# Exchanging two PSUM evacuations between VectorE and ScalarE in the attention stage, and issuing three loads earlier

## The chip, the cores and the metric

One Trainium2 chip; the same program runs on eight of its cores, each on its own 1,024 of 8,192 rows of x. The metric is the device time of the slowest core in microseconds.

## The reference

Per row of x (4,096 wide), with xn the layer norm of x:

```
c  = conv1d(xn, width 3, 4096 -> 3072) + conv_b ; q, k, v = split(c)      # each 1024 wide
qh, kh, vh = q wq + bq, k wk + bk, v wv + bv                              # 16 heads of 64
p  = softmax(causal(qh kh^T / 8))     within blocks of 128 rows
s  = ((p vh) wo + bo) proj_w + proj_b                                      # 4096 wide
w  = top-8 of softmax(xn rw^T + rb), 64 experts
g  = silu(xn * sum(w) + w expert_bias)
out = x + s * g
```

## The kernel before

The program is written out by hand: every `@PE`, `@DV`, `@AC`, `@GP`, `@SY` function adds a piece to the instruction stream of TensorE, VectorE (DVE), ScalarE (ACT), GpSimd (POOL) or SyncE (SP), in the order of the text, and the engines meet only at semaphores.

Stages, one after the other: layer norm, transposes and router (to about 210 us), convolution (to about 1,220 us, L632 and L647), the three projections q, k, v (L682, L694, L716, L726, to about 1,308 us), attention (L755 to L924, 1,308 to 1,576 us), final projection with gate and output (L965 to the end).

Attention has 8 blocks of 128 rows and 16 heads. A unit of work Q is four heads of one block, so Q runs from 0 to 31; eight consecutive Q (two blocks) form a block pair `bp`, and there are four pairs. For each Q:

- `st_quad` (PE, L755 and L758): scores of four heads into half of pS, then the mask is added by one more matmul. Semaphore cS.
- `st_dve1` (DVE, L765): negated row maximum. cNM.
- `st_exp` (ACT, L772): Exp with that maximum as bias, in place in pS. cEXP.
- `st_dve2` (DVE, L779, L783, L787): row sums, reciprocal, four multiplies that write bf16. cPS.
- `st_pt` (PE, L799): transposes into pPT. cPT.
- `st_pte` (ACT, L809): copies pPT to SBUF (pTs). cPTe.
- `st_ot` (PE, L823): four matmuls with vh into pOT. cOT.
- `st_ote` (DVE, L839): four tensor_scalar adds of the bias bv, 64x128 each, into oT2. cOTe.

Within a pair the step of Q puts these on the engines, in this order. PE: quad(Q), pt(Q-1), ot(Q-2). DVE: dve2(Q-1), dve1(Q), and after them ote(Q-3). ACT: pte(Q-2), exp(Q). After the last Q of a pair (Qm) come dve2(Qm), the last copies pte(Qm-1) and pte(Qm), the last pt and ot, and three ote. Only then do the 128 matmuls of the output projection of that pair (L913, pWO) start, since they wait for all its ote (cOTe); ACT evacuates them in eight instructions (L924, cEV5), counted on the PE side by cPE5. pS, pPT and pOT have two halves each, used by Q modulo 2.

Every `@AC` function that has ACTIVATE instructions shows one ACT_TABLE_LOAD in the trace.

Around the end of attention: POOL loads proj_w in eight pieces (L602, pw), the first when cS reaches 32 (the quad of Q = 31 is done), each next one when the piece before it has landed. SP waits at L934 for cEV5 = 32 and cOT = 32, loads proj_b (L936, into the first row of x6[0]'s buffer), waits at L937 for cPB = 2 (proj_b split into a high and a low bf16 part by ACT L945 and DVE L950), and then loads the x of tile 0 and tile 1 (L938 and L939, 2 MB each, x6[0] and x6[1]). PE starts L965 at cPB = 2 and takes one proj_w piece after another. The last tiles are paced by x loads that are issued one tile ahead (L1071).

Of the kernel before, what the change touches and what calls it, by code (L numbers as in the profile page):

```python
# [9 lines left out]
AF = mybir.ActivationFunctionType  # L10
ALU = mybir.AluOpType
# [71 lines left out]
def build_program():  # L83
    nc = bass.Bass("TRN2", target_bir_lowering=False)

    d_x = nc.dram_tensor("x", [NT + 2, D], F32, kind="ExternalInput").ap()
# [21 lines left out]
    with contextlib.ExitStack() as es:  # L108
        def sb(name, shape, dt):
            return es.enter_context(nc.sbuf_tensor(name, shape, dt))  # L110
# [7 lines left out]
        t_bvT = sb("tBvT", [64, 16], F32)  # L118
# [17 lines left out]
        def bfv(off, cols, parts=128):  # L136
            return AL[0:parts, off:off + cols]

        def f32v(off, cols_f32, parts=128):
            return AL[0:parts, off:off + 2 * cols_f32].bitcast(F32)  # L140
# [38 lines left out]
        pTs = bfv(A_PT, 1024)  # L179
        pbf = bfv(A_PBF4, 1024)  # L180
        x6 = [f32v(A_X6A, 4096), f32v(A_X6B, 4096)]
# [64 lines left out]
        SY, GP, PE, DV, AC = blk.sync, blk.gpsimd, blk.tensor, blk.vector, blk.scalar  # L246
# [15 lines left out]
        @SY  # L262
        def _(e):
            sCONST.add(e.dma_start(out=t_cbT[:], in_=d_cb), 16)
            sCONST.add(e.dma_start(out=t_bqT[:], in_=d_bq), 16)
            sCONST.add(e.dma_start(out=t_bkT[:], in_=d_bk), 16)
            sCONST.add(e.dma_start(out=t_bvT[:], in_=d_bv), 16)
            sCONST.add(e.dma_start(out=t_boT[:], in_=d_bo), 16)
            sCONST.add(e.dma_start(out=t_rbT[:], in_=d_rb), 16)
            sCONST.add(e.dma_start(out=i64v, in_=d_i64), 16)  # L270
            sCONST.add(e.dma_start(out=i128f, in_=d_i128), 16)
            sXA.add(e.dma_start(out=xA[0:64, :], in_=d_rw), 16)
# [463 lines left out]
        with nc.psum_tensor("pS", [128, 2 * 512], F32) as p_S, \  # L736
# [7 lines left out]
            def st_quad(e, Q):  # L744
                b, qi = divmod(Q, 4)
                sB = 512 * (Q % 2)
                if Q == 0:
                    e.wait_ge(cEV3.h, EV3ALL)
                    e.wait_ge(sCST2.h, 48)
                if Q >= 2:  # L750
                    e.wait_ge(cPS.h, 4 * (Q - 1))
                for i in range(4):
                    head = 4 * qi + i
                    off = 1024 * head + 128 * b
                    e.matmul(p_S[:, sB + 128 * i:sB + 128 * i + 128],  # L755
                             qhT[:, off:off + 128], khT[:, off:off + 128],
                             start=(i == 0), stop=False)
                cS.add(e.matmul(p_S[:, sB:sB + 512], t_i128[:], t_mask4[:],  # L758
                                start=False, stop=True), 1)

            def st_dve1(e, Q):
                e.wait_ge(cS.h, Q + 1)
                if Q >= 2:
                    e.wait_ge(cEXP.h, Q - 1)
                cNM.add(e.reduce_max(nmax[Q % 2][:],  # L765
                                     p_S[:, 512 * (Q % 2):512 * (Q % 2) + 512],
                                     axis=AX.X, negate=True), 1)

            def st_exp(e, Q):
                e.wait_ge(cNM.h, Q + 1)  # L770
                sB = 512 * (Q % 2)
                cEXP.add(e.activation(p_p[:, sB:sB + 512], p_S[:, sB:sB + 512],  # L772
                                      AF.Exp, bias=nmax[Q % 2][:]), 1)
# [30 lines left out]
            def st_pte(e, Q):  # L804
                e.wait_ge(cPT.h, Q + 1)
                if Q >= 2:
                    e.wait_ge(cOT.h, Q - 1)
                sB = 512 * (Q % 2)
                cPTe.add(e.activation(pTs[:, sB:sB + 512], p_pT[:, sB:sB + 512],  # L809
                                      AF.Copy), 1)  # L810

            def st_ot(e, Q):
                b, qi = divmod(Q, 4)
# [16 lines left out]
            def st_ote(e, Q):  # L830
                b, qi = divmod(Q, 4)
                e.wait_ge(cOT.h, Q + 1)
                if b // 2 >= 2:
                    e.wait_ge(cPE5.h, 8 * (b // 2 - 1))
                sB = 512 * (Q % 2)
                dst = oT2[(b // 2) % 2]
                for i in range(4):
                    head = 4 * qi + i
                    cOTe.add(e.tensor_scalar(  # L839
                        dst[0:64, head, 128 * (b % 2):128 * (b % 2) + 128],  # L840
                        p_oT[0:64, sB + 128 * i:sB + 128 * i + 128],
                        t_bvT[:, head:head + 1], None, ALU.add), 1)

            for bp in range(4):
                Qs = list(range(8 * bp, 8 * bp + 8))
                for Q in Qs:
                    @PE
                    def _(e, Q=Q, Qs=Qs):
                        st_quad(e, Q)
                        if Q - 1 in Qs:  # L850
                            st_pt(e, Q - 1)
                        if Q - 2 in Qs:
                            st_ot(e, Q - 2)

                    @DV
                    def _(e, Q=Q, Qs=Qs):
                        if Q - 1 in Qs:
                            st_dve2(e, Q - 1)
                        st_dve1(e, Q)

                    @AC
                    def _(e, Q=Q, Qs=Qs):
                        if Q - 2 in Qs:
                            st_pte(e, Q - 2)
                        st_exp(e, Q)

                    @DV
                    def _(e, Q=Q, Qs=Qs):
                        if Q - 3 in Qs:
                            st_ote(e, Q - 3)  # L870

                Qm = Qs[-1]

                @DV
                def _(e, Qm=Qm):
                    st_dve2(e, Qm)

                @AC
                def _(e, Qm=Qm):
                    st_pte(e, Qm - 1)  # L880

                @PE
                def _(e, Qm=Qm):
                    st_pt(e, Qm)
                    st_ot(e, Qm - 1)

                @AC
                def _(e, Qm=Qm):
                    st_pte(e, Qm)

                @PE
                def _(e, Qm=Qm):
                    st_ot(e, Qm)

                @DV
                def _(e, Qm=Qm):
                    st_ote(e, Qm - 2)
                    st_ote(e, Qm - 1)
                    st_ote(e, Qm)

                @PE
                def _(e, bp=bp, Qm=Qm):
                    e.wait_ge(cOTe.h, 32 * (bp + 1))
                    if bp == 0:
                        e.wait_ge(sWO.h, 16)
                    src = oT2[bp % 2]
                    for c in range(8):
                        wB = 512 * (c % 2)
                        if c >= 2:
                            e.wait_ge(cEV5.h, 8 * bp + c - 1)  # L910
                        ins = None
                        for hk in range(16):
                            ins = e.matmul(p_wo_t[:, wB:wB + 256],  # L913
                                           wob[:, hk, 128 * c:128 * c + 128],
                                           src[0:64, hk, 0:256],
                                           start=(hk == 0), stop=(hk == 15))
                        cPE5.add(ins, 1)

                @AC
                def _(e, bp=bp):  # L920
                    for c in range(8):
                        e.wait_ge(cPE5.h, 8 * bp + c + 1)
                        wB = 512 * (c % 2)
                        cEV5.add(e.activation(aoT[:, c, 256 * bp:256 * bp + 256],  # L924
                                              p_wo_t[:, wB:wB + 256], AF.Identity,
                                              bias=t_boT[:, c:c + 1]), 1)
# [4 lines left out]
        with nc.psum_tensor("pPr", [128, 8 * 512], F32) as p_pr:  # L931
            @SY
            def _(e):
                e.wait_ge(cEV5.h, 32)  # L934
                e.wait_ge(cOT.h, 32)
                sPB32.add(e.dma_start(out=pbf32, in_=d_pb), 16)  # L936
                e.wait_ge(cPB.h, 2)  # L937
                sX6A.add(e.dma_start(out=x6[0], in_=d_x[1:129, :]), 16)  # L938
                sX6B.add(e.dma_start(out=x6[1], in_=d_x[129:257, :]), 16)  # L939

            @AC
            def _(e):
                e.wait_ge(sPB32.h, 16)
                e.wait_ge(cEV5.h, 32)
                cPB.add(e.copy(pbhi[0:1, :], pbf32[0:1, :]), 1)  # L945

            @DV
# [212 lines left out]
if __name__ == "__main__":  # L1160
    nc = build_program()
    print("instructions:", nc.n_instructions())
```

## Time and profile before

| | |
|---|---|
| median of 2 runs | 1893.26 us (1889.58 and 1896.95) |
| profiled execution | 1901.35 us; span of its slowest core 1899.8 us |
| spans of the eight cores in it | 1869.2 to 1899.8 us |
| busy share of the span, PE / DVE / ACT / POOL | 81% / 21% / 20% / 12% |
| attention stage in the span | about 1,308 to 1,576 us |

The shares are averages over stages with different limits: PE is at nine tenths or more through the convolution, and at five to eight tenths in the slices of attention and of the final projection. So the attention stage has to be read in its own timeline, by the start of one operation that recurs in each step, and by what ends each wait. In a timeline row the bracket gives the idle time of that engine before the instruction and what ended it.

### The profile page before, as it was taken

The numbers are of one execution on the slowest core, as the hardware profiler recorded it, in microseconds if no ns is written. First come the engines' busy times: TensorE is split into PE (matmuls) and PEld (weight loads), VectorE is DVE, ScalarE is ACT, GpSimd is POOL, SyncE is SP. The second block draws the span as 40 slices with busy tenths as digits, with TensorE's granted clock in tenths as the row PEclk, the third lists the DMA queues.
The fourth block names the chain that finished last, engine by engine and source line by source line (L and its number), as shares of the span: only waits on it lengthen the run. The fifth ranks groups of instructions, "written<-read, shape, count | busy, mean of one in ns | idle before, by whom it ended". The sixth has DMA issues, their size and how long they took to land.

```text
span 1899.8 us, 17839 instructions; the slowest of 8 cores (1869.2 to 1899.8 us)
## 1 busy us (share of the span) xinstructions
PE 1534.9 (81%) x7424; PEld 726.5 (38%) x7424; DVE 393.7 (21%) x644; ACT 383.6 (20%) x453; POOL 229.3 (12%) x180
## 2 busy tenths in 40 slices
PE   0344799999999999999999999887756775876771
PEld 0344344444444444444444444333434442221220
DVE  2776200000000000000000000002354241454664
ACT  1443000000000000000000000496354341423322
POOL 0000111111111111111111111000000000132343
PEclk9867899999999999999999999997555556887775
DMA  5998666666666666666666666522000037134234
GB/s 138 213 244 167 78 78 75 72 76 77 78 78 76 72 74 78 78 78 76 74 74 77 78 78 73 94 48 41 1 1 1 1 69 182 27 123 142 89 99 167
DMA packets 230821, 163.62 MB, mean 86 GB/s; under 512 B 74691, under 2 KB 222403, under 8 KB 226499
## 3 DMA queue, kind: packets, MB, share of 16 engines
q0 software_dynamic: 155472, 92.97, 38.6%
q1 hardware_dynamic: 75270, 69.50, 14.1%
q8 instruction: 60, 0.98, 0.2%
q14 instruction: 19, 0.16, 0.0%
HBM read 220.69 MB, written 16.78 MB: 125 GB/s over the span
## 4 chain that ended last, share of the span: by engine, by line
PE 61%; DMA 12%; DVE 9%; ACT 7%; POOL 4%; issue 3%; SPq 3%; POOLq 0%; DVEq 0%; ACTq 0%
PE pCv L632 53%; DMA AL<-x 7%; PE pWO L913 4%; DMA AL<-pw 4%; POOL AL L1050 2%; ACT AL L694 2%; POOL AL L1053 2%; SPq L416 2%; DVE AL L787 1%; PE pQ L716 1%; DVE tStat L320 1%; DVE tRs L779 1%; ACT L694 1%; DVE tSc L765 1%; DVE AL L839 1%
## 5 line engine op out<-in xcount | busy, mean ns | idle before, releaser
L632 PE MATMUL pCv<-AL 128*128 128x512 bf16 x4608 | 1000.6, 379 | 1.0 <-DVE tWmT L550 1.0
L632 PEld LDWEIGHTS pCv<-AL 128*128 128x128 bf16 x4608 | 449.5, 98 | 551.9 <-issue 1.3
L765 DVE TENSOR_REDUCE tSc<-pS 128x1 f32<-128x512 f32 x32 | 21.8, 682 | 1187.7 <-PE pS L758 1187.7
L575 POOL DMA_DIRECT2D AL<-cw x144 | 125.9, 875 | 1054.0 <-PE pCv L632 860.6
L647 ACT ACTIVATE AL<-pCv,tCbT 128x512 bf16<-128x512 f32 x48 | 29.1, 688 | 889.2 <-PE pCv L632 889.2
L454 PE MATMUL pLgT<-AL 128*64 128x128 bf16 x768 | 60.3, 258 | 129.3 <-DMA AL<-AL 129.3
L982 PE MATMUL pPr<-AL 128*128 128x512 bf16 x448 | 120.9, 418 | 22.3 <-DVE AL L1030 22.3
L913 PE MATMUL pWO<-AL 64*128 64x256 bf16 x512 | 109.8, 416 | 5.7 <-DVE AL L839 5.7
L454 PEld LDWEIGHTS pLgT<-AL 128*64 128x64 bf16 x768 | 59.3, 138 | 130.2 <-issue 130.2
L913 PEld LDWEIGHTS pWO<-AL 64*128 64x128 bf16 x512 | 74.5, 146 | 40.1 <-issue 6.6
L982 PEld LDWEIGHTS pPr<-AL 128*128 128x128 bf16 x448 | 42.2, 104 | 96.8 <-issue 63.5
L799 PE MATMUL pPT<-tI,AL 128*128 128x128 bf16 x128 | 18.7, 300 | 72.9 <-DVE AL L787 72.9
L1050 POOL TENSOR_TENSOR AL<-AL 128x1536 f32<-128x1536 f32 x8 | 45.5, 5686 | 187.8 <-ACT AL L1042 187.8
L682 PE MATMUL pQ<-AL 128*128 128x512 bf16 x256 | 57.7, 379 | 10.3 <-ACT AL L694 7.5
L1011 PE MATMUL pPr<-AL,tWmT 64*128 64x512 bf16 x64 | 29.5, 562 | 36.7 <-ACT AL L1001 36.7
L320 DVE BATCH_NORM_STATS2 tStat<-AL 128x6 f32<-128x512 f32 (+1 forms) x72 | 43.5, 677 | 17.8 <-DMA AL<-x 17.8
L1060 DVE TENSOR_TENSOR AL<-AL 128x2560 f32<-128x2560 f32 x8 | 45.9, 5741 | 2.5 <-ACT AL L1044 2.5
L1030 DVE TENSOR_TENSOR AL<-AL,pPr 128x512 f32<-128x512 f32 x64 | 39.0, 680 | 32.7 <-PE pPr L1011 31.6
L799 PEld LDWEIGHTS pPT<-tI,AL 128*128 128x128 bf16 x128 | 11.1, 126 | 87.2 <-issue 87.2
L602 POOL DMA_DIRECT2D AL<-pw x8 | 4.3, 533 | 327.6 <-PE pS L758 258.8
L965 PE MATMUL pPr<-AL 128*128 128x512 bf16 x64 | 20.0, 486 | 29.1 <-DMA AL<-pw 29.1
L1025 DVE TENSOR_SCALAR AL<-AL,tMrv,tSc 128x4096 f32<-128x4096 f32 x8 | 19.3, 2413 | 114.2 <-DMA AL<-x 114.0
(95 smaller groups left out, 878.4 us busy)
## 6 DMA issues: line engine op xcount, KB each, us to landing
AL<-cw POOLq DMA_DIRECT2D x144, 512.0 KB, 5.9
AL<-x SPq DMA_DIRECT2D x16, 2048.0 KB, 15.9
out<-AL SPq DMA_DIRECT2D x8, 2048.0 KB, 9.1
AL<-pw POOLq DMA_DIRECT2D x8, 1024.0 KB, 8.5
AL<-wq POOLq DMA_DIRECT2D x1, 2048.0 KB, 19.8
AL<-wk POOLq DMA_DIRECT2D x1, 2048.0 KB, 15.9
AL<-wv POOLq DMA_DIRECT2D x1, 2048.0 KB, 15.7
AL<-wo POOLq DMA_DIRECT2D x1, 2048.0 KB, 16.4
```

The source lines that it names most:

```text
L320: ins = e.bn_stats(t_stat[rows, sb0 + 6 * c:sb0 + 6 * c + 6], xt[rows, 512 * c:512 * c + 512])
L454: ins = e.matmul(p_lgT[:, 128 * j:128 * j + 128], lhsT_t[:, 64 * dcc:64 * dcc + 64], src_[:, o:o + 128], start=(j % 4 == 0 and p == 0 and ...
L575: sCWs[gi % 4].add(e.dma_start(out=cwr[:, gi % 4, :].rearrange("p (g f) -> p g f", g=8), in_=d_cw[s, g].rearrange("g p f -> p g f")), 16)
L632: ins = e.matmul(p_cv[:, 512 * (bs + 2 * sub + hf): 512 * (bs + 2 * sub + hf) + 512], lhsT, xnTh[:, o:o + 512], start=(step == 0), stop=(s ...
L682: ins = e.matmul(p_q3[:, 512 * (bs + hf):512 * (bs + hf) + 512], lhsT, cvT[:, 8 * m + kc, 512 * hf:512 * hf + 512], start=(kc == 0), stop= ...
L694: cEV3.add(e.activation(outT[0:64, 1024 * head + 512 * hf: 1024 * head + 512 * hf + 512], p_q3[64 * hh:64 * hh + 64, 512 * (bs + hf):512 * ...
L765: cNM.add(e.reduce_max(nmax[Q % 2][:], p_S[:, 512 * (Q % 2):512 * (Q % 2) + 512], axis=AX.X, negate=True), 1)
L913: ins = e.matmul(p_wo_t[:, wB:wB + 256], wob[:, hk, 128 * c:128 * c + 128], src[0:64, hk, 0:256], start=(hk == 0), stop=(hk == 15))
L982: e.matmul(p_pr[:, 512 * seg:512 * seg + 512], aoT[:, kc, 128 * tt:128 * tt + 128], pwv[:, kc, 512 * seg:512 * seg + 512], start=(kc == 0) ...
L1030: cGI.add(e.tensor_add(gw[:, 512 * seg:512 * seg + 512], gw[:, 512 * seg:512 * seg + 512], p_pr[:, 512 * seg:512 * seg + 512]), 1)
L1050: cPL.add(e.tensor_mul(s6[tt % 2][:, 0:1536], s6[tt % 2][:, 0:1536], gw[:, 0:1536]), 1)
L1060: dedge(e, e.tensor_mul(s6[tt % 2][:, 1536:4096], s6[tt % 2][:, 1536:4096], gw[:, 1536:4096]))
```

## The change

`st_pte`, the copy of pPT to SBUF, goes from ACT (activation Copy) to DVE (tensor_copy). `st_ote`, the four bias adds, go from DVE (tensor_scalar) to ACT (activation Identity with a bias pointer). The order within a step becomes: DVE dve2(Q-1), dve1(Q), pte(Q-2); ACT exp(Q), ote(Q-3). At the end of a pair, the two last copies are on DVE and the three last ote are one function on ACT.

SP's waits for cEV5 and cOT at L934 become one for cPE3 = 24 (the last matmul of the q, k, v projections); proj_b and x6[1] are loaded right behind it, and x6[0] alone stays behind cPB = 2. ACT's split of proj_b waits for cPE5 = 32 in place of cEV5 = 32.

```diff
--- before.py
+++ after.py
@@ -806,8 +806,7 @@
                 if Q >= 2:
                     e.wait_ge(cOT.h, Q - 1)
                 sB = 512 * (Q % 2)
-                cPTe.add(e.activation(pTs[:, sB:sB + 512], p_pT[:, sB:sB + 512],
-                                      AF.Copy), 1)
+                cPTe.add(e.tensor_copy(pTs[:, sB:sB + 512], p_pT[:, sB:sB + 512]), 1)
 
             def st_ot(e, Q):
                 b, qi = divmod(Q, 4)
@@ -836,10 +835,10 @@
                 dst = oT2[(b // 2) % 2]
                 for i in range(4):
                     head = 4 * qi + i
-                    cOTe.add(e.tensor_scalar(
+                    cOTe.add(e.activation(
                         dst[0:64, head, 128 * (b % 2):128 * (b % 2) + 128],
                         p_oT[0:64, sB + 128 * i:sB + 128 * i + 128],
-                        t_bvT[:, head:head + 1], None, ALU.add), 1)
+                        AF.Identity, bias=t_bvT[:, head:head + 1]), 1)
 
             for bp in range(4):
                 Qs = list(range(8 * bp, 8 * bp + 8))
@@ -857,15 +856,12 @@
                         if Q - 1 in Qs:
                             st_dve2(e, Q - 1)
                         st_dve1(e, Q)
+                        if Q - 2 in Qs:
+                            st_pte(e, Q - 2)
 
                     @AC
                     def _(e, Q=Q, Qs=Qs):
-                        if Q - 2 in Qs:
-                            st_pte(e, Q - 2)
                         st_exp(e, Q)
-
-                    @DV
-                    def _(e, Q=Q, Qs=Qs):
                         if Q - 3 in Qs:
                             st_ote(e, Q - 3)
 
@@ -874,9 +870,6 @@
                 @DV
                 def _(e, Qm=Qm):
                     st_dve2(e, Qm)
-
-                @AC
-                def _(e, Qm=Qm):
                     st_pte(e, Qm - 1)
 
                 @PE
@@ -884,7 +877,7 @@
                     st_pt(e, Qm)
                     st_ot(e, Qm - 1)
 
-                @AC
+                @DV
                 def _(e, Qm=Qm):
                     st_pte(e, Qm)
 
@@ -892,7 +885,7 @@
                 def _(e, Qm=Qm):
                     st_ot(e, Qm)
 
-                @DV
+                @AC
                 def _(e, Qm=Qm):
                     st_ote(e, Qm - 2)
                     st_ote(e, Qm - 1)
@@ -931,17 +924,16 @@
         with nc.psum_tensor("pPr", [128, 8 * 512], F32) as p_pr:
             @SY
             def _(e):
-                e.wait_ge(cEV5.h, 32)
-                e.wait_ge(cOT.h, 32)
+                e.wait_ge(cPE3.h, 24)
                 sPB32.add(e.dma_start(out=pbf32, in_=d_pb), 16)
+                sX6B.add(e.dma_start(out=x6[1], in_=d_x[129:257, :]), 16)
                 e.wait_ge(cPB.h, 2)
                 sX6A.add(e.dma_start(out=x6[0], in_=d_x[1:129, :]), 16)
-                sX6B.add(e.dma_start(out=x6[1], in_=d_x[129:257, :]), 16)
 
             @AC
             def _(e):
                 e.wait_ge(sPB32.h, 16)
-                e.wait_ge(cEV5.h, 32)
+                e.wait_ge(cPE5.h, 32)
                 cPB.add(e.copy(pbhi[0:1, :], pbf32[0:1, :]), 1)
 
             @DV
```

## Rows read from the trace of the kernel before

**Rows 1.** Page, part 4, shares of the chain that ended last, by line.
```profile
PE pCv L632 53%; DMA AL<-x 7%; PE pWO L913 4%; DMA AL<-pw 4%; POOL AL L1050 2%; ACT AL L694 2%; POOL AL L1053 2%; SPq L416 2%; DVE AL L787 1%; PE pQ L716 1%; DVE tStat L320 1%; DVE tRs L779 1%; ACT L694 1%; DVE tSc L765 1%; DVE AL L839 1%
```

**Rows 2.** Timeline, fourth block pair, its first two steps: start, us, engine, line, operation [idle].
```profile
1509.80 0.69 DVE L765 TENSOR_REDUCE tSc<-pS 128x1 f32<-128x512 f32 x1 [28.75 <-PE pS L758]
...
1514.82 0.68 DVE L765 TENSOR_REDUCE tSc<-pS 128x1 f32<-128x512 f32 x1
...
1515.58 1.28 ACT L772 ACT_TABLE_LOAD   x1 [3.05 <-DVE tSc L765]
...
1516.87 0.66 ACT L772 ACTIVATE pS<-pS,tSc 128x512 f32<-128x512 f32 x1
...
1519.83 0.68 DVE L765 TENSOR_REDUCE tSc<-pS 128x1 f32<-128x512 f32 x1
```

**Rows 3.** Timeline, the same pair, one later step.
```profile
1534.97 0.68 DVE L765 TENSOR_REDUCE tSc<-pS 128x1 f32<-128x512 f32 x1
...
1535.57 1.11 DVE L839 TENSOR_SCALAR AL<-pOT,tBvT 64x128 bf16<-64x128 f32 x4
...
1535.75 0.66 ACT L772 ACTIVATE pS<-pS,tSc 128x512 f32<-128x512 f32 x1 [1.23 <-DVE tSc L765]
...
1535.82 0.64 PE L823 MATMUL pOT<-AL 128*64 128x128 bf16 x4
...
1536.43 1.28 ACT L809 ACT_TABLE_LOAD   x1
...
1536.60 0.67 DVE L779 TENSOR_REDUCE tRs<-pS 128x4 f32<-128x512 f32 x1
...
1537.73 1.13 DVE L787 TENSOR_SCALAR AL<-pS,tRr 128x128 bf16<-128x128 f32 x4 [0.18 <-DVE tRr L783]
...
1538.78 0.68 DVE L765 TENSOR_REDUCE tSc<-pS 128x1 f32<-128x512 f32 x1
```

**Rows 4.** Timeline, the end of that pair.
```profile
1546.56 1.12 DVE L839 TENSOR_SCALAR AL<-pOT,tBvT 64x128 bf16<-64x128 f32 x4 [1.20 <-PE pOT L823]
...
1547.82 27.46 PE L913 MATMUL pWO<-AL 64*128 64x256 bf16 x128 [1.44 <-DVE AL L839]
```

**Rows 5.** Groups by shape: line, engine, operation, shapes, count, busy us, mean ns, idle.
```profile
L809 ACT ACT_TABLE_LOAD x32 | 41.1, 1283 | 6.5 <-PE pPT L799 6.1
...
L772 ACT ACT_TABLE_LOAD x8 | 10.3, 1283 | 18.0 <-DVE tSc L765 18.0
...
L647 ACT ACTIVATE AL<-pCv,tCbT 128x512 bf16<-128x512 f32 x48 | 29.1, 688 | 889.2 <-PE pCv L632 889.2
...
L694 ACT ACTIVATE AL<-pQ,tBqT 64x512 bf16<-64x512 f32 x32 | 21.9, 683 | 0.7
...
L924 ACT ACTIVATE AL<-pWO,tBoT 128x256 bf16<-128x256 f32 x32 | 15.2, 474 | 77.2 <-PE pWO L913 77.2
...
L489 DVE COPY AL<-pLgt 128x512 f32<-128x512 f32 x1 | 0.7, 691 | 2.2 <-PE pLgt L481 2.2
```

**Rows 6.** Chain that ended last, in order of time: start, us, what.
```profile
1538.11 9.10 DMA AL<-pw
...
1565.16 8.10 DMA AL<-pw
...
1592.10 17.95 DMA AL<-pw
...
1610.58 10.33 DMA AL<-pw
...
1621.05 3.37 PE pPr L965 x8
```

**Rows 7.** Timeline between the fourth pair and the projection.
```profile
1575.99 0.22 SPq L936 DMA_DIRECT2D AL<-pb  x1
...
1581.58 1.28 ACT L945 ACT_TABLE_LOAD   x1 [5.72 <-DMA AL<-pb]
...
1591.07 0.37 SPq L938 DMA_DIRECT2D AL<-x  x1
```

## The prediction

> **What bounds the kernel now.** I read the page first, its chain that ended last. Convolution matmuls are 53% of it and the change does not touch them; the rest is many small shares, of which the proj_w load has 4% and the attention lines one or two per cent each [rows 1]. So the change acts on attention (some 267 us) and on the loads behind it, and I read both in the timeline, by the start of dve1 (L765), once per step.
>
> Two lengths of a step stand in one block pair. The second step takes 1519.83 - 1514.82 = 5.01 us, the first 5.02 [rows 2]. In it nothing overlaps: dve1 ends at 1515.50, ACT starts a table load at 1515.58, Exp starts at 1516.87, and DVE can only sum when Exp is over. A later step takes 1538.78 - 1534.97 = 3.81 us [rows 3]: Exp starts 0.10 after dve1 ends, since the load of that ACT function stands at its first ACTIVATE, the copy of pPT, which comes before Exp and runs while DVE is busy with dve2. DVE has no gap to speak of there; the four ote adds (1.11 us) fill the time in which it would wait for Exp.
>
> The reader is to see in the groups by shape where the loads stand: 32 at L809 (once per copy) and only 8 at L772, for the two steps of each of four pairs that begin with Exp [rows 5]. The load at L772 begins after the wait for dve1, not during it: its row has 3.05 us idle that ended with tSc L765 [rows 2].
>
> Behind attention the chain runs through the proj_w pieces: the first is issued at 1538.11, when quad 31 is done, the last is issued at 1610.58 and lands for PE at 1621.05 [rows 6]. The seventh took 17.95 us where others take 8.1 to 9.1, because the two x loads were issued at 1591.07 and right after [rows 7], 4 MB on the same DMA engines.
>
> **The change part by part.** *Copy to DVE, ote to ACT, the load ahead of Exp.* Now Exp is the first ACTIVATE of every ACT function in a step, so the load stands between dve1 and Exp in all eight steps of a pair. The serial path of a step is then that of [rows 2]: 5.01 us. I take this value, since it is a measured step of the same kernel with the same order dve1, load, Exp, dve2, dve1. The Trainium skill says of the compiler's loads that they are placed per block (ScalarE activation tables: per-element evaluation and per-set limits, section Table sets in the compiler and the runtime); the counts in [rows 5] agree.
>
> The copy on DVE costs about 0.69, by a DVE copy of 128x512 f32 out of PSUM [rows 5] (that one writes f32; bf16 is not shown to be slower). It lies between dve1(Q) and dve2(Q), where DVE waits over 2.0 us for load and Exp (1516.87 + 0.66 - 1515.50): hidden. If that cover were gone it would cost 0.69 a step.
>
> Four Identity with bias, 64x128 each: no such row. 128x256 takes 474 ns and 128x512 688 ns, so 0.84 ns a column; 64 partitions cost as much as 128 (683 ns) [rows 5]. For 128 columns: 474 - 107 = 367 ns, with a small gap 0.385, four are 1.54 us. The bounds: from below what DVE takes for the same four, 1.11 us or 0.28 each [rows 3]; from above the 474 ns of twice the columns. ACT in a step: 0.08 + 1.28 + 0.67 + 1.54 = 3.6 us, under 5.01; even four at 474 ns give 3.9. Hidden in the steady part. What is queued behind it is Exp of the next step, due 5.01 later. On PE, ot(Q-2) now waits for a copy that ends 0.7 after dve1(Q); quad(Q+1) queued behind it ends at most 3.9 us after the start of dve1(Q) (0.68 + 0.69 + 0.2 + 2.3, the last from the fourth-pair sum below) and is wanted at 5.01: 1.1 us spare.
>
> Sum of a pair: seven intervals of dve1. Before 1538.78 - 1509.80 = 28.98 [rows 2, 3]; after 7 x 5.01 = 35.07; +6.1 us.
>
> *The end of a pair.* Before, from the last dve1 (1538.78) to the first pWO matmul (1547.82) 9.04 us [rows 3, 4]. After, counted from that dve1: load and Exp until 0.76 + 1.28 + 0.67 = 2.71; ote(Qm-3) until 4.25; the load of the last ACT function until 5.55; three ote of 1.54 until 10.17; pWO 0.14 later (before, it came 0.14 after the end of ote), 10.3. The pOT of Qm is ready earlier, at about 7.8, where it was before (ote began at 1546.56, 7.78 after [rows 4]): the load before the last copy is gone, one before Exp has come. So +1.3 us, ACT bound. With 0.28 for one Identity ote ends at 7.8 + 1.11 and pWO starts at 9.05: 0; with 0.474, 11.65: +2.6.
>
> *Three pairs* lie ahead of the fourth: 3 x (6.1 + 1.3) = +22.2 us. The bounds of the tail make this 18.3 to 26.1.
>
> *Fourth pair.* What counts is quad 31, since it releases proj_w. Its predecessor on PE is the pOT group of the copy. Before, that group started at 1535.82 and POOL issued 2.29 later, at 1538.11, 28.31 after the pair's start [rows 2, 3, 6]. After: dve1 of Q = 30 starts at 6 x 5.01 = 30.06, ends 30.74, copy until 31.43, pOT at 31.65, issue at 33.95. +5.6 us. Sum at the first proj_w piece: +27.8 us (bounds 24 to 32).
>
> *The early loads.* proj_b and x6[1] go out at about 1,308 us, with the v projection done and only attention running, which loads nothing by then but proj_w at its end: no cost. The proj_b split no longer waits the 5.6 us for its load (1575.99 to 1581.58), so it is done 9.5 us after attention's last evacuation (1591.07 - 1581.58) [rows 7]; PE does not gain by it, as the proj_w pieces bound PE. x6[0] alone now meets the sixth or seventh piece. Two x loads made the seventh 17.95 instead of about 8.4, +9.5, and the eighth 10.33, part of it theirs. Half the bytes, half of it: about -5 us. Bounds: 0 (one load costs all) and -9.5 (the one left is hidden).
>
> *ACT's wait on cPE5 = 32*: nothing; it stands behind L924 in ACT's order anyhow. From the last proj_w piece to the end nothing changes: the x loads there keep their order.
>
> Sum: +27.8 - 5 = +22.8 us. On the profiled execution, 1901.35 becomes 1924.1; that execution is 8 us above the median, so on the median 1893.3 becomes 1916.1 us, +1.2%.
>
> **The rivals.** *Loads off the path.* If the loads ran during the wait, or only when the table set changes, a step would be 5.01 - 1.28 = 3.73 us, against 3.81. Then the DVE's lighter work shows: 5 x 0.08 in a pair, 1.6 us in all, at the tails about 1.3 less each (5 us), and the 5 of the x load: 1882 us, faster than before, not slower. It decides in the first three steps of a pair. For it: both functions of a step may share a set, as Copy and Exp do (one load for both). Against it: the load is repeated each step though the same two functions alternate, and it starts after the wait. 7%.
>
> *A second load, for Identity after Exp.* No row shows the two in one function. ACT in a step would be 3.6 + 1.28 = 4.9, still under 5.01, and each tail 1.3 longer: three times, +4: 1920 us. Its upper end: Identity at 474 ns as well makes ACT 5.2 a step and Exp late by 0.2: +6 more. The Trainium skill says that cheap functions, identity among them, are in every set (ScalarE: Activation LUTs, section Table sets: the hidden batching unit), which speaks against it. 8%.
>
> *ACT becomes the bound.* If an Identity of 128 columns cost as much as one of 512 (0.69) and a second load came, ACT would need 0.08 + 1.28 + 0.67 + 1.28 + 2.76 = 6.1 us a step: 27 steps at +1.1 and tails +5 each, 1960 us, slower by over 2%. It decides where four Identity exceed 1.7 us with a second load, or 3.0 without one. Against it the slope of [rows 5]. 5%.
>
> *A pause behind each load.* In the trace Exp begins 0.01 us after the load ends (1515.58 + 1.28 = 1516.86) [rows 2]. With a pause as long as the load behind each, 27 steps on the path (7 in each of three pairs, 6 in the fourth) would add 27 x 1.28 = 35 us, 1951 us. That is what the Trainium skill gives for a switch of set, 1283 ns plus a drain of about 1380 (ScalarE: Activation LUTs, section What ACT_TABLE_LOAD costs). The load's 1283 ns agree with [rows 5], the drain does not appear in [rows 2]. 1%.
>
> *The early x load brings nothing*, because the load that stays costs as much as both: 1921 us. 9%.
>
> **How the numbers follow.** The forecast has 70%: 1916 us, own range 1906 to 1923 (tail bounds -4 and +4, load bounds, and a few us between executions, as the two runs before are 7 apart). With the second load and the useless early load its upper end is 1926; the faster rival stays outside below. The range is 1904 to 1926. A measurement of this kernel can tell about 2% from no change, 38 us: 1855 and 1931. Faster by over 2% 1%, since no case reaches it; slower by over 2% 8%: the bound on ACT, the pause, and the top of the second load; within 2% 91%.
>
> **What would show it.** Right: 32 table loads at L772 and none at the copy; dve1 starting every 5.0 us through a whole pair; 1.3 to 1.5 us of DVE idle before each row sum, after the copy; pWO 45 us after the first dve1 of a pair, where it was 38; the seventh proj_w piece near 13 us. Wrong: steps of 3.7 us; table loads between Exp and Identity; Identity above 0.45 us; ACT without idle time; a first proj_w piece less than 24 us later than before.

## The result and the profile after

The changed kernel takes 1912.6 us (median of 11 executions) where the kernel before takes 1890.3 in the same sessions; the ratio is 1.0106, with a 95% interval of 1.0060 to 1.0151. So it is about 20 us slower: the whole interval lies above 1, though the size is under the 2% that I took as the smallest difference to call. The forecast was 1.2%.

In the profiled execution of the changed kernel, cores 2 and 3 lost some 50 us in the convolution, which the change does not touch, at a lower granted clock (0.838 over the span, core 5 0.859). All rows of it below are therefore of core 5. The lines of the kernel after have other numbers than those before: the copy stays L809, but ote is L838 (before L839), ot L822 (L823), the output projection L906 (L913), its evacuation L917 (L924).

The groups by shape on core 5 (line, engine, operation, shapes, count | busy us, mean ns | idle before, releaser):

```profile
L772 ACT ACT_TABLE_LOAD x32 | 41.1, 1283 | 76.5 <-DVE tSc L765 76.5
...
L838 ACT ACTIVATE AL<-pOT,tBvT 64x128 bf16<-64x128 f32 x128 | 35.6, 355 | 2.0 <-PE pOT L822 1.9
...
L838 ACT ACT_TABLE_LOAD x4 | 5.1, 1283 | 0.1
...
L917 ACT ACT_TABLE_LOAD x4 | 5.1, 1283 | 15.3 <-PE pWO L906 15.3
```

These answer to [rows 5]. Of the 40 table loads of the attention steps, 32 stood at the copy and 8 at Exp; now there are 36: 32 stand at Exp (L772), all behind a wait for dve1 (76.5 us of idle time, released by tSc), and 4 at the three last ote (L838), one for each pair. None stands between Exp and Identity.

One step of the first pair in the timeline on core 5 (start, us, engine, line, operation [idle before]):

```profile
1330.29 0.68 DVE L765 TENSOR_REDUCE tSc<-pS 128x1 f32<-128x512 f32 x1
...
1330.89 0.68 DVE L809 CAST AL<-pPT 128x512 bf16<-128x512 f32 x1
...
1331.05 1.28 ACT L772 ACT_TABLE_LOAD   x1 [2.01 <-DVE tSc L765]
...
1331.85 0.61 PE L822 MATMUL pOT<-AL 128*64 128x128 bf16 x4 [0.65 <-DVE AL L809]
...
1332.34 0.66 ACT L772 ACTIVATE pS<-pS,tSc 128x512 f32<-128x512 f32 x1
...
1332.93 1.11 ACT L838 ACTIVATE AL<-pOT,tBvT 64x128 bf16<-64x128 f32 x4
...
1333.10 0.69 DVE L779 TENSOR_REDUCE tRs<-pS 128x4 f32<-128x512 f32 x1 [1.54 <-ACT pS L772]
...
1334.25 1.13 DVE L787 TENSOR_SCALAR AL<-pS,tRr 128x128 bf16<-128x128 f32 x4 [0.18 <-DVE tRr L783]
...
1335.30 0.68 DVE L765 TENSOR_REDUCE tSc<-pS 128x1 f32<-128x512 f32 x1
```

It answers to [rows 3]. The step is 1335.30 - 1330.29 = 5.01 us, where it was 3.81, and equal to the second step of [rows 2]. After dve1 comes the load, then Exp, and DVE waits 1.54 us for them in spite of the copy (0.68) that now fills part of that time. The four Identity take 1.11 us and end long before ACT is wanted again.

The end of that pair, on the same core:

```profile
1345.66 0.68 DVE L765 TENSOR_REDUCE tSc<-pS 128x1 f32<-128x512 f32 x1
...
1346.42 1.28 ACT L772 ACT_TABLE_LOAD   x1 [2.37 <-DVE tSc L765]
...
1349.43 1.28 ACT L838 ACT_TABLE_LOAD   x1
...
1350.72 1.12 ACT L838 ACTIVATE AL<-pOT,tBvT 64x128 bf16<-64x128 f32 x4
...
1352.30 2.23 ACT L838 ACTIVATE AL<-pOT,tBvT 64x128 bf16<-64x128 f32 x8 [0.46 <-PE pOT L822]
...
1354.78 15.52 PE L906 MATMUL pWO<-AL 64*128 64x256 bf16 x72 [1.47 <-ACT AL L838]
```

From the last dve1 to pWO it is 9.12 us, where [rows 3, 4] gave 9.04 for the fourth pair. The same pair on the same core took 9.09 before, so the end of a pair is as long as it was. ACT waits 0.46 us for pOT ahead of the last eight Identity, so ACT alone does not bound it.

The first, sixth, seventh and eighth proj_w pieces, on core 5 (the bracket of a row is the time that the piece before it took, so 11.82 belongs to the sixth and 9.29 to the seventh):

```profile
1563.63 0.56 POOL L602 DMA_DIRECT2D AL<-pw  x1 [284.26 <-PE pS L758]
...
1608.00 0.53 POOL L602 DMA_DIRECT2D AL<-pw  x1 [8.28 <-DMA AL<-pw]
...
1620.35 0.53 POOL L602 DMA_DIRECT2D AL<-pw  x1 [11.82 <-DMA AL<-pw]
...
1630.17 0.53 POOL L602 DMA_DIRECT2D AL<-pw  x1 [9.29 <-DMA AL<-pw]
```

They answer to [rows 6]: 1563.63 less the 1534.61 of the same core before is 29 us, of which 25.4 belong to attention on this core and the rest to the earlier stages of the two executions. The sixth and seventh together take 21.1 us, two undisturbed ones 16.7; before, the two from the sixth on took 8.4 and 17.4 on this core.

### The profile page after: what moved, and what is told of

It is laid out like the page before. It is cut to its first block, busy times and chain, and to the rows that moved or that the text cites. A ratio compares the mean times of both kernels' runs of the same rounds, so it can differ in the third digit from the quotient of the medians.

```text
span 1945.7 us, 17834 instructions; the slowest of 8 cores (1886.8 to 1945.7 us)
## 1 busy us (share of the span) xinstructions
PE 1588.0 (82%) x7424; PEld 739.1 (38%) x7424; DVE 381.2 (20%) x548; ACT 393.5 (20%) x545; POOL 229.3 (12%) x180
## 4 chain that ended last, share of the span: by engine, by line
PE 63%; DMA 10%; ACT 8%; DVE 7%; POOL 4%; issue 4%; SPq 3%; POOLq 0%; DVEq 0%; ACTq 0%
PE pCv L632 54%; DMA AL<-x 6%; PE pWO L906 4%; DMA AL<-pw 4%; POOL AL L1042 2%; ACT AL L694 2%; POOL AL L1045 2%; PE pQ L716 1%; DVE tStat L320 1%; SPq L416 1%; DVE AL L787 1%; ACT L694 1%; DVE tSc L765 1%; DVE tRs L779 1%; ACT pS L772 1%
## 5 line engine op out<-in xcount | busy, mean ns | idle before, releaser
L632 PE MATMUL pCv<-AL 128*128 128x512 bf16 x4608 | 1054.3, 394 | 1.0 <-DVE tWmT L550 1.0
L632 PEld LDWEIGHTS pCv<-AL 128*128 128x128 bf16 x4608 | 462.2, 100 | 593.1 <-issue 177.7
L974 PE MATMUL pPr<-AL 128*128 128x512 bf16 x448 | 117.8, 410 | 11.4 <-DVE AL L1022 11.4
L906 PE MATMUL pWO<-AL 64*128 64x256 bf16 x512 | 109.8, 415 | 5.7 <-ACT AL L838 5.7
L906 PEld LDWEIGHTS pWO<-AL 64*128 64x128 bf16 x512 | 73.2, 144 | 41.3 <-issue 6.5
L682 PE MATMUL pQ<-AL 128*128 128x512 bf16 x256 | 57.7, 379 | 10.3 <-ACT AL L694 7.5
L1042 POOL TENSOR_TENSOR AL<-AL 128x1536 f32<-128x1536 f32 x8 | 45.5, 5687 | 160.4 <-ACT AL L1034 160.4
L772 ACT ACT_TABLE_LOAD x32 | 41.1, 1283 | 76.5 <-DVE tSc L765 76.5
L320 DVE BATCH_NORM_STATS2 tStat<-AL 128x6 f32<-128x512 f32 (+1 forms) x72 | 43.6, 677 | 16.7 <-DMA AL<-x 16.6
L1045 POOL TENSOR_TENSOR AL<-AL 128x1536 f32<-128x1536 f32 x7 | 42.0, 5999 | 0.0
## 6 DMA issues: line engine op xcount, KB each, us to landing
AL<-wv POOLq DMA_DIRECT2D x1, 2048.0 KB, 15.7
```

Source lines behind the costliest of these rows:

```text
L320: ins = e.bn_stats(t_stat[rows, sb0 + 6 * c:sb0 + 6 * c + 6], xt[rows, 512 * c:512 * c + 512])
L632: ins = e.matmul(p_cv[:, 512 * (bs + 2 * sub + hf): 512 * (bs + 2 * sub + hf) + 512], lhsT, xnTh[:, o:o + 512], start=(step == 0), stop=(s ...
L682: ins = e.matmul(p_q3[:, 512 * (bs + hf):512 * (bs + hf) + 512], lhsT, cvT[:, 8 * m + kc, 512 * hf:512 * hf + 512], start=(kc == 0), stop= ...
L906: ins = e.matmul(p_wo_t[:, wB:wB + 256], wob[:, hk, 128 * c:128 * c + 128], src[0:64, hk, 0:256], start=(hk == 0), stop=(hk == 15))
L974: e.matmul(p_pr[:, 512 * seg:512 * seg + 512], aoT[:, kc, 128 * tt:128 * tt + 128], pwv[:, kc, 512 * seg:512 * seg + 512], start=(kc == 0) ...
L1042: cPL.add(e.tensor_mul(s6[tt % 2][:, 0:1536], s6[tt % 2][:, 0:1536], gw[:, 0:1536]), 1)
```

## A measure that the convolution does not disturb

The spans of the cores differ by more than the effect, for two reasons outside it: the convolution (up to 50 us) and the last stage, which takes anything from 238 to 269 us in kernels with the same instructions there, nearly alike within a pair of cores. So beside each ratio I give three stretches from the POOL rows of the profiled execution, medians over eight cores: **A** from the issue of the wo load to the first proj_w piece (the last 32 us of the projections, then attention up to quad 31; it is the same on all cores within 0.4 us), **B** from there to POOL's first gate multiplication, **C** from there to the end of the span.

| kernel | A us | B us | C us | ratio to before (95%) |
|---|---|---|---|---|
| before | 259.7 | 96.6 | 247.2 | |
| changed | 284.9 | 89.2 | 243.2 | 1.0106 (1.0060 to 1.0151) |
| e1 early loads only | 259.7 | 92.1 | 250.9 | 0.9975 (0.9938 to 1.0012) |
| e2 exchange only | 284.9 | 97.3 | 244.5 | 1.0141 (1.0075 to 1.0207) |
| e3 ote ahead of Exp | 262.1 | 91.5 | 263.9 | none |
| e10 the same, again | 262.1 | 91.4 | 241.1 | 1.0011 (0.9968 to 1.0054) |
| e4 one ACT function a pair | 251.7 | 90.3 | 255.7 | 0.9951 (0.9928 to 0.9974) |
| e5 before, Exp ahead of copy | 295.8 | 97.6 | 241.5 | 1.0267 (1.0217 to 1.0316) |
| e6 before, one ACT function | 250.7 | 94.4 | 241.3 | 0.9965 (0.9921 to 1.0010) |
| e8 both x loads early | 259.6 | 86.5 | 242.0 | 0.9968 (0.9923 to 1.0012) |
| e9 last stage, one function | 259.7 | 94.1 | 218.9 | 0.9896 (0.9813 to 0.9979) |
| e7 all together | 249.0 | 85.4 | 219.5 | 0.9765 (0.9708 to 0.9822) |

## Experiments: the two parts of the change apart

**Early loads only** (e1). The kernel before with SP's and ACT's new waits (ACT's, on cPE5, is not shown):

```diff
-                e.wait_ge(cEV5.h, 32)
-                e.wait_ge(cOT.h, 32)
+                e.wait_ge(cPE3.h, 24)
                 sPB32.add(e.dma_start(out=pbf32, in_=d_pb), 16)
+                sX6B.add(e.dma_start(out=x6[1], in_=d_x[129:257, :]), 16)
                 e.wait_ge(cPB.h, 2)
                 sX6A.add(e.dma_start(out=x6[0], in_=d_x[1:129, :]), 16)
-                sX6B.add(e.dma_start(out=x6[1], in_=d_x[129:257, :]), 16)
```

> The kernel before with the second part of the change alone: proj_b and x6[1] loaded behind the q, k, v projections, ACT's wait on cPE5. Theory (the load that stays costs about half of what two cost): attention steps stay at 3.81 us, the sixth and seventh proj_w pieces together exceed two undisturbed ones by 4 to 5 us in place of 9 to 10, and the kernel is 4 to 6 us faster than before (about 0.3%). Rival (one x load delays proj_w as much as two): 0 us. Rival (the early x load costs something in attention): POOL's wait for the first proj_w piece grows above 258.8 us.

A is unchanged to 0.1 us, so the early load costs attention nothing. B is 4.5 us shorter. The ratio, 0.9975, says the same size (4.7 us) but its interval includes 1.

**The exchange only** (e2). The changed kernel with SP and ACT waiting as before.

> The changed kernel with the loads as before: only the exchange of the two evacuations. Theory: steps of 5.01 us, POOL's wait from the last weight load to the first proj_w piece 284 us (before 258.8), seventh proj_w piece near 17.5 us again, and 25 us slower than before (1.3%). If the early loads were worth nothing, the same time as the changed kernel.

A is 25.2 us longer than before, the same as in the changed kernel; B is 97.3, as before. The ratio is 1.0141, +27 us. So the two parts add: one costs 25 us, the other gives 5 to 8 back.

**Both x loads early** (e8), to see whether the disturbance goes with the bytes. proj_b gets a buffer of its own, so that x6[0] need not wait for it. Shown is the difference to e1:

```diff
-        pbf32 = f32v(A_X6A, 4096, 1)
+        pbf32 = f32v(A_SA, 4096, 1)
...
+                sX6A.add(e.dma_start(out=x6[0], in_=d_x[1:129, :]), 16)
                 sX6B.add(e.dma_start(out=x6[1], in_=d_x[129:257, :]), 16)
-                e.wait_ge(cPB.h, 2)
-                sX6A.add(e.dma_start(out=x6[0], in_=d_x[1:129, :]), 16)
```

> The kernel before with both x loads and proj_b behind the projections (proj_b in a buffer of its own), so no x load meets proj_w. Theory (the disturbance goes with the bytes): all proj_w pieces at 8 to 9 us; from the first proj_w piece to the first gate multiplication 87 us, against 96.7 before and 92 with one load early; 8 us faster than before. Rival (proj_w does not bound the start of the final stage once one load is early): 92 us as with one.

B is 96.6, 92.1 and 86.5 us with two, one and no x load beside proj_w: -4.5 and then -5.6. With none, POOL's rows (core 0) show all pieces alike:

```profile
1590.09 0.53 POOL L602 DMA_DIRECT2D AL<-pw  x1 [8.83 <-DMA AL<-pw]
...
1598.93 0.53 POOL L602 DMA_DIRECT2D AL<-pw  x1 [8.32 <-DMA AL<-pw]
```

The rival, that proj_w no longer bounds the start of the last stage, falls. The ratio is 0.9968, 6 us where 8 were expected, and its interval just includes 1; that the loads help rests on B. There all twelve rows of the table agree: 94.1 to 97.6 us with both x loads beside proj_w (five kernels), 89.2 to 92.1 with one (five), 86.5 and 85.4 with none.

## Experiments: what lengthens the step

My theory is that the table load ahead of Exp sets the step. The rivals are the exchange itself (the copy in DVE's order, PE's wait for it, Identity on ACT) and a second load for Identity.

**ote ahead of Exp** (e3, and once more as e10). All instructions stay on their engines; only ACT's order changes:

```diff
-                        st_exp(e, Q)
                         if Q - 3 in Qs:
                             st_ote(e, Q - 3)
+                        st_exp(e, Q)
```

> The changed kernel with one exchange in ACT's order: in each step ote(Q-3) comes ahead of exp(Q). The same instructions on the same engines; only the place of the table load moves, to the first ote. Theory (the load ahead of Exp is what costs): the load runs while DVE does dve2 and dve1, steps with an ote ahead last 3.7 to 3.9 us and only the first three of a pair 5.0; POOL's wait falls from 284 to about 263 us, and the kernel is 0 to 3 us faster than the one before. Rival (the copy on DVE, or PE's wait for it, is what lengthens the step): steps stay near 5.0 us and the time near that of the changed kernel (+1.1%).

> The kernel with ote(Q-3) ahead of exp(Q) once more, with more rounds, for a ratio: attention 2.5 us longer than before (262.1 against 259.7 us from the wo load to the first proj_w piece), the early loads 5 us shorter: 2 to 3 us faster than before, ratio 0.998 to 0.999.

The starts of dve1 in the first pair (timeline, DVE, core 0 of e3), third to sixth:

```profile
1350.07 0.68 DVE L765 TENSOR_REDUCE tSc<-pS 128x1 f32<-128x512 f32 x1
...
1355.08 0.68 DVE L765 TENSOR_REDUCE tSc<-pS 128x1 f32<-128x512 f32 x1
...
1358.81 0.68 DVE L765 TENSOR_REDUCE tSc<-pS 128x1 f32<-128x512 f32 x1
...
1362.54 0.68 DVE L765 TENSOR_REDUCE tSc<-pS 128x1 f32<-128x512 f32 x1
```

The third step, without an ote, still takes 5.01 us; from the fourth on a step takes 3.73. A falls from 284.9 to 262.1 us: 22.8 of the 25.2 us are back through the place of one instruction. The four executions of e3 lie too far apart for a ratio (1897.8 to 2096.6 us); e10 gives 1.0011 with an interval from 0.9968 to 1.0054, which neither confirms the 2 to 3 us of gain that I expected nor excludes them. A and B are as expected.

**One ACT function for a pair** (e4). The changed kernel, order unchanged, with the eight steps and the last three ote in one function (shown are the added lines; the nine functions that they replace go):

```diff
+                @AC
+                def _(e, Qs=Qs, bp=bp):
+                    for Q in Qs:
+                        st_exp(e, Q)
+                        if Q - 3 in Qs:
+                            st_ote(e, Q - 3)
+                    for Q in Qs[-3:]:
+                        st_ote(e, Q)
```

> The changed kernel with all attention steps of a pair written into one ACT function, in unchanged order. Theory (one table load per function, none needed between Exp and Identity): one load for a pair in place of nine, every step 3.73 us (5.01 - 1.28), and the end of the pair 1.3 us shorter than before; per pair 7 x 3.73 - 28.98 = -2.9 and -1.3, so three pairs and the start of proj_w give -15 us against before, with the early loads -20 us (1.0% faster). Rival (a load for each change between Exp and Identity): two loads a step, steps of 5 us or more. Rival (the exchange itself costs): steps above 4 us without a load on the path.

Groups by shape on ACT, and two starts of dve1 with the Exp and Identity between them (core 6):

```profile
L772 ACT ACT_TABLE_LOAD x4 | 5.1, 1283 | 5.9 <-DVE tSc L765 5.9
...
L838 ACT ACTIVATE AL<-pOT,tBvT 64x128 bf16<-64x128 f32 x128 | 35.2, 357 | 7.9 <-PE pOT L822 7.6 <-issue 0.3
```

```profile
1327.47 0.68 DVE L765 TENSOR_REDUCE tSc<-pS 128x1 f32<-128x512 f32 x1
...
1328.25 0.66 ACT L772 ACTIVATE pS<-pS,tSc 128x512 f32<-128x512 f32 x1 [2.03 <-DVE tSc L765]
...
1328.84 1.11 ACT L838 ACTIVATE AL<-pOT,tBvT 64x128 bf16<-64x128 f32 x4
...
1331.20 0.68 DVE L765 TENSOR_REDUCE tSc<-pS 128x1 f32<-128x512 f32 x1
```

One load a pair, none for Identity, and a step of 3.73 us = 5.01 - 1.28, with the copy on DVE and ote on ACT. Both rivals fall: with the exchange and no load on the path a step takes 3.73, except the last of each pair (4.08). The kernel is 0.5% faster than before. I had expected 1.0%: A fell by 8.0 us against before and not by 15, because the one load of the pair stands behind the first dve1, so the first step stays at 4.95 to 5.02 (1.28 a pair forgotten), and one step of seven takes 4.08.

That last step is 0.35 us longer in every kernel with the exchange (5.36 beside 5.01 in the changed kernel and e2, 4.08 beside 3.73 in e3, e10 and e4) and in none with the evacuations as before and the copy ahead of Exp. In the changed kernel its row sum starts 1.11 us after Exp does, and 0.76 in the other steps, though the Exp row is as long (0.66). What delays it is not shown.

**The load ahead of Exp with no exchange** (e5). The kernel before, in which only the copy and Exp change places in ACT's order:

```diff
-                        if Q - 2 in Qs:
-                            st_pte(e, Q - 2)
                         st_exp(e, Q)
+                        if Q - 2 in Qs:
+                            st_pte(e, Q - 2)
```

> The kernel before with one exchange in ACT's order and nothing else: exp(Q) ahead of pte(Q-2). The copy stays on ACT, ote on DVE, the loads late. Theory (the place of the table load sets the step, whichever engine has which evacuation): every step at least 5.0 us; here the copy comes 2.04 us after dve1 instead of at once, so pOT and quad(Q+1) behind it on PE end near 5.3 us after the start of dve1(Q), and the step is 5.3 to 5.4. POOL's wait for proj_w about 290 us (before 258.8), the kernel about 30 us slower than before (1.6%). Rival (the exchange of engines is what costs): steps of 3.8 us, no change.

Two steps in DVE's timeline (core 7):

```profile
1322.40 0.69 DVE L765 TENSOR_REDUCE tSc<-pS 128x1 f32<-128x512 f32 x1 [0.25 <-PE pS L758]
...
1327.64 0.69 DVE L765 TENSOR_REDUCE tSc<-pS 128x1 f32<-128x512 f32 x1
...
1333.00 0.69 DVE L765 TENSOR_REDUCE tSc<-pS 128x1 f32<-128x512 f32 x1 [0.25 <-PE pS L758]
```

Steps of 5.24 and 5.36 us, some of them ended by PE (0.25 us for the scores, as expected from the late copy), and a kernel 2.7% slower than before, without any exchange. The direction and the step are as expected; A grew by 36 us and not by 31. The trace shows where: the seven steps of a pair are 7.8 to 8.05 us longer than before, which makes 23.7 in three pairs; from the last dve1 to pWO it is 10.2 to 10.3 us in place of 9.0 to 9.1, another 3.6, which I had not counted; and the fourth pair up to the first proj_w piece takes 37.2 in place of 28.3.

**One ACT function, before's assignment** (e6), the same edit as e4 on the kernel before.

> The kernel before, its copies still on ACT and its ote on DVE, with the ACT steps of a pair in one function; late loads. Theory: one load a pair, waiting for the first dve1, so a first step of 5.0 us, a second of 3.73, and the rest at 3.81, where DVE is busy throughout; the end of the pair 1.3 us shorter. Per pair -1.3 and -1.3, with the fourth POOL's wait falls by 9 us to about 250 us; the kernel 9 us faster than before (0.5%). Beside the same with the exchange (250.9 us measured), the exchange itself is worth 0 to 2 us once the loads are out of the way.

A is 250.7 us; with the exchange (e4) it was 251.7. So once the loads are out of the way the exchange is worth nothing, or costs 1 us. Steps are 3.80 us with ote on DVE and 3.73 without, but the last step of a pair with the exchange is the 4.08 of e4, which takes the gain back. The ratio, 0.9965, includes 1 by a hair.

## Experiments: the version that beats both

**All together** (e7): e4, both x loads early, and the same merging of ACT functions in the q, k, v projections and in the last stage (the functions are collected in a list and called in one):

```diff
-                @AC
+                @acl.append
                 def _(e, tt=tt):
...
+            @AC
+            def _(e):
+                for f in acl:
+                    f(e)
```

> The changed kernel, the ACT steps of a pair in one function, the ACT parts of the q, k, v projections in one function (16 steps of 4.12 us bound by ACT with a load of 1.28 each, PE needs 3.61: about -7.5 us), those of the final stage in one function (a load before each silu lies on the chain of each tile: up to -9 us), and both x loads early with proj_b in a buffer of its own (-3 us more). With the 9 us that the one-function version of attention gained: 1862 to 1868 us, 1.5% faster than before. If Silu and Copy share no set, the loads of the final stage stay and 9 us of it do not come.

Its ratio is 0.9765 (0.9708 to 0.9822), 44 us faster than before, which is 16 us more than the 1.5% that I expected. The projections gave 11.3 us (from the wk load to the first dve1 88.5 us, before 99.8; expected 7.5). A is 2.7 us shorter than in e4 because it holds the last of these; attention itself gave the 8 us of e4. B is 11.2 us shorter, where 5 and 3 were expected. The last stage gave most of the surplus: C fell from 247.2 to 219.5, where I had put 9 us; compared between cores whose x loads took equally long (see the last section), it fell by about 21.

**The last stage alone** (e9), on the kernel before.

> The kernel before with the ACT parts of the final stage in one function, nothing else. In the version with everything together a tile of the final stage took 28.2 us on a core where it took 31.8 before: 1.3 us for the table load ahead of the silu, and 2.55 us because POOL's first multiplication then runs in 3.45 us, ahead of DVE's, in place of 6.00 beside it. Expected here: tiles 3.5 us shorter, the stage 20 to 25 us shorter, the kernel 1.1 to 1.3% faster than before. If the shorter tiles came from the other edits of that version, only 9 us.

C is 218.9 us on every core within 3.4, and the ratio 0.9896, just short of the 1.1 to 1.3% expected. So the gain is of that stage. One tile of it before, on core 6 (timeline):

```profile
1746.01 1.28 ACT L1042 ACT_TABLE_LOAD   x1 [4.09 <-DVE AL L1030]
...
1747.30 1.49 ACT L1042 ACTIVATE AL<-AL 128x1536 f32<-128x1536 f32 x1
...
1748.84 2.82 DVE L1035 TENSOR_TENSOR AL<-AL 128x2560 f32<-128x2560 f32 x1
...
1748.93 6.00 POOL L1050 TENSOR_TENSOR AL<-AL 128x1536 f32<-128x1536 f32 x1 [19.79 <-ACT AL L1042]
...
1754.90 6.00 POOL L1053 TENSOR_TENSOR AL<-AL 128x1536 f32<-128x1536 f32 x1
...
1760.97 0.34 SPq L1071 DMA_DIRECT2D out<-AL  x1
```

And in e9, on the same core:

```profile
1763.32 1.48 ACT L1044 ACTIVATE AL<-AL 128x1536 f32<-128x1536 f32 x1 [6.05 <-DVE AL L1032]
...
1764.95 3.44 POOL L1052 TENSOR_TENSOR AL<-AL 128x1536 f32<-128x1536 f32 x1 [19.32 <-ACT AL L1044]
...
1766.14 4.94 DVE L1037 TENSOR_TENSOR AL<-AL 128x2560 f32<-128x2560 f32 x1
...
1768.36 6.00 POOL L1055 TENSOR_TENSOR AL<-AL 128x1536 f32<-128x1536 f32 x1
...
1774.43 0.34 SPq L1073 DMA_DIRECT2D out<-AL  x1
```

Before, DVE's addition starts 0.09 us ahead of POOL's multiplication, which then takes 6.00 us. Without the load POOL starts 1.19 us ahead of DVE; it takes 3.44 and DVE's takes 4.94 where it took 2.82. POOL is on the chain of the tile and DVE's addition (L1035, in e9 L1037) is not: the store of the finished tile, and behind it the x load for the next, goes out 0.07 us after POOL's second row ends in both kernels. So the load was worth 1.28 + 2.56 = 3.84 us a tile, and most tiles are that much closer: 31.8 us apart before, 27.9 to 29.3 in e9, where the longer ones wait longer for x. The Trainium skill says that DVE and GpSimd share one pair of SBUF ports under an exclusive lock, that a DVE instruction with two SBUF inputs contends for it with a GpSimd instruction that reads SBUF, and that the order of issue decides who is blocked (SBUF — State Buffer, section Who interferes with whom). These rows agree: POOL loses 2.56 us where DVE's addition has 2.73 still to run when POOL starts, and in e9 DVE loses 2.12 us where POOL has 2.25 still to run.

## Why the prediction was right

- **The load ahead of Exp, 5.01 us a step**: right, and shown from three sides. Taking the load away (e4) or moving it (e3) removes the 1.28 us, and moving it there without the exchange (e5) brings it. A step measured in the kernel before was the right price. The last step of each pair took 5.36, which I had not foreseen and no run explains.
- **One load for Exp and Identity**: right; the 8% rival of a second load is out, since L838 has 4 loads, each at the head of a function. The pause behind the load is out too: Exp starts 1.29 us after the load does.
- **Copy 0.69, hidden**: measured 0.68, hidden.
- **The tail, +1.3 us a pair**: the mis-sized term. I took 1.54 us for four Identity from the slope between 256 and 512 columns and a gap; they take 1.11, since each starts before the one before it has ended (355 ns each in their rows, starts 0.25 apart). It was the lower bound of the text: on the same core the tails are 9.12, 9.01 and 9.06 us where they were 9.09, 8.98 and 9.06, so the term is 0. Three pairs of 1.3 less, three steps of 0.35 more and 0.2 more in the fourth pair (+5.8 for the +5.6 of the text; its first step takes 5.30) give 27.8 - 3.9 + 1.05 + 0.2 = 25.2, which is what A shows.
- **The early loads, -5 us**: e1 gave -4.5 in B and the changed kernel -7.4; B differs by up to 5 us on a core between e3 and e10, the same kernel, so the two agree. The disturbance fell on the sixth and seventh piece, 4.4 us together on core 5, where the text looked for it in one of the two ("the seventh proj_w piece near 13 us").
- **Sum**: predicted +27.8 - 5 = +22.8; by the stretches +25.2 - 7.4 = +17.8; by the ratio about +20, with an interval from 11 to 29. Both terms came out about 2.5 us lower than forecast, so no two errors cancel in the total.
- **Loads off the path (7%)**: it did not happen, but its step was right: 3.73 us, seen in e3 and e4. Its sum of 1882 us was for loads that no step waits for; e4 has 0.9951.

## What to carry to other kernels

Where a trace shows an ACT table load at the head of each function, its place in the function is a scheduling decision: put an instruction that is ready early ahead of the one that others wait for, or write the steps into one function, so that the load is paid once. Before moving work between engines, look at which of its rows stands on the serial chain; here the exchange of 1.1 and 0.7 us of work was worth nothing, and the load that it moved was worth most of 25 us. A step of the kernel itself that already has the new order, such as the first steps of a pair, gives a better price than any sum of parts.

## What the runs showed that I had not expected

- A POOL multiplication of 128x1536 f32 takes 3.44 us when it starts ahead of a DVE tensor_tensor and 6.00 when it starts 0.09 us behind it. A delay of 1.28 us upstream thus cost 3.8 us a tile.
- Four ACTIVATE of 64x128 out of PSUM take 1.11 us together at 355 ns each, while those of 64x512 with a pointer bias in [rows 5] do not overlap (683 ns each, their starts 0.71 apart, four in 2.81 us).
- The last stage takes from 238 to 269 us at the same instructions, nearly alike within a pair of cores: in the kernel before 266 to 268 us on cores 0 and 1 and 240 on cores 6 and 7. The trace shows that the x loads make the difference. From the issue of a tile's x load (L1076) to the DVE instruction that uses it (L1025), cores 6 and 7 take 11.9 us on the mean of six tiles, cores 0 and 1 16.1 and 16.3. In the version with everything together cores 6 and 7 are the long pair (15.7 and 15.2 us, C 240 and 238) beside 12.0 to 12.4 us and C of 218 to 221 on the others; in e9 no core is (12.1 to 12.8 us). What picks the pair was not tried.
